# 33 places for the weighted one-hots with few signals, the counts' store beside the next tile's sums, and gathers without steps, in a two-layer graph kernel on one core

## What is computed

```
a     = h[src] @ Ws.T + h[dst] @ Wd.T + emb_rel[etype] @ Wr.T
e     = leaky_relu(a @ attn_fc2_w.T, 0.01)
w     = exp(e - segment_max(e, dst)[dst])
alpha = w / segment_sum(w, dst)[dst]
agg   = segment_sum(alpha * h[src], dst)        # h where a node has no edge
x1    = layernorm(x + agg + h @ loop_weight)
# twice, from h = x1:
msg   = (rel_embed[etype] + h[src]) @ W_r
h     = rrelu(segment_sum(msg, dst) * deg**-0.5 + where(no edge, h @ W_el, h @ W_sl))
out   = layernorm(x1 + h)
```

## Time and profile before

| | us |
|---|---|
| median of 3 runs | 2790.08 (2789.8 to 2791.62) |
| profiled execution, span from the first to the last instruction | 3256.5 |
| busy in it: PE / PEld / DVE / ACT / POOL | 2357.3 / 1900.0 / 2054.9 / 1230.7 / 1582.9 |
| its longest groups: gathers L587, comparisons L1142 of the counts, closing sums L979, sums L904 | 1537.7 / 564.1 / 551.4 / 548.8 |
| its mean granted clock of TensorE | 0.860 of full speed |

### The profile page before, as it was taken

One profiled execution on the slowest core, in us unless ns is written; L12 is line 12 of the kernel. 1 busy time (PEld: TensorE's weight loads), 2 busy tenths in 40 slices (PEclk: granted clock), 3 DMA queues, 4 the chain that ended last, 5 costly groups with the idle time before them and its releaser, 6 DMA issues.

```text
span 3256.5 us, 45435 instructions
## 1 busy us (share of the span) xinstructions
PE 2357.3 (72%) x16208; PEld 1900.0 (58%) x16208; DVE 2054.9 (63%) x4582; ACT 1230.7 (38%) x3215; POOL 1582.9 (49%) x1672
## 2 busy tenths in 40 slices
PE   1136666666766767677677777777777799999999
PEld 0125544545555556556556566566565677688887
DVE  4647766767767767767767777777676745632333
ACT  1125544444444544444444544444444432300000
POOL 4634666666666666666666666666656500000000
PEclk9877877878788888888887888888888899999999
DMA  6323444344444444454444444444444335466665
GB/s 182 113 78 112 131 136 123 118 148 128 123 155 132 121 155 133 122 156 135 125 157 135 126 141 142 140 139 129 154 130 121 93 128 170 142 214 214 210 212 168
DMA packets 184631, 463.49 MB, mean 142 GB/s; under 512 B 86337, under 2 KB 113785, under 8 KB 164578
## 3 DMA queue, kind: packets, MB, share of 16 engines
q1 hardware_dynamic: 116050, 339.10, 30.9%
q0 software_dynamic: 53600, 114.17, 14.2%
q10 hardware_dynamic: 14752, 7.26, 0.9%
HBM read 362.54 MB, written 97.84 MB: 141 GB/s over the span
## 4 chain that ended last, share of the span: by engine, by line
PE 60%; issue 12%; another core or an unknown queue 11%; DVE 8%; ACT 8%; DMA 1%; SPq 0%; ACTq 0%; DVEq 0%
PE pair L979 16%; PE bank L904 15%; PE pair L834 8%; PE bank L865 8%; DVE arena L1142 4%; ACT arena L609 4%; PE pair L811 2%; PE pair L803 2%; PE pair L801 1%; PE pair L802 1%; ACT arena L706 1%; PE pair L952 1%; ACT L653 1%; PE bank L857 1%
## 5 line engine op out<-in xcount | busy, mean ns | idle before, releaser
L587 POOL DMA_INDIRECT arena<-rows,srcw x1617 | 1537.7, 951 | 1000.7 <-issue 411.3
L1142 DVE TENSOR_TENSOR arena<-bank,idx 128x2000 bf16<-128x2000 bf16 (+3 forms) x700 | 564.1, 855 | 289.9 <-PE pair L834 218.7
L904 PE MATMUL bank<-arena 128*125 128x130 f32 x3300 | 548.8, 340 | 54.2 <-ACT arena L706 30.1
L904 PEld LDWEIGHTS bank<-arena 128*125 128x125 f32 x3300 | 534.0, 241 | 62.6 <-ACT arena L706 35.0
L979 PE MATMUL pair<-arena 125*125 125x384 bf16 x3285 | 551.4, 326 | 1.6 <-DVE arena L1343 1.6
L834 PE MATMUL pair<-arena 128*128 128x250 bf16 x2500 | 400.5, 312 | 201.7 <-issue 87.6
L609 ACT ACTIVATE arena<-pair 99x264 f32<-99x264 f32 (+2 forms) x410 | 282.3, 711 | 674.1 <-PE pair L834 306.6
L706 ACT ACTIVATE arena<-arena,wexp 128x128 f32<-128x128 bf16 x1650 | 496.1, 387 | 105.7 <-PE bank L904 61.8
L979 PEld LDWEIGHTS pair<-arena 125*125 125x125 bf16 x3285 | 447.4, 136 | 103.3 <-issue 8.4
L834 PEld LDWEIGHTS pair<-arena 128*128 128x128 bf16 x2500 | 260.2, 110 | 313.9 <-issue 187.5
L1112 DVE TENSOR_TENSOR arena<-arena,bank 128x4224 bf16<-128x4224 int16 x150 | 344.2, 2350 | 1.7
(11 more groups left out here) (250 smaller groups left out, 2329.6 us busy)
## 6 DMA issues: line engine op xcount, KB each, us to landing
arena<-counts SPq DMA_DIRECT2D x106, 812.5 KB, 4.4
counts<-arena SPq DMA_DIRECT2D x50, 1562.5 KB
arena<-dst SPq DMA_DIRECT2D x50, 1056.0 KB
arena<-etype SPq DMA_DIRECT2D x50, 1056.0 KB
arena<-rows,srcw POOLq DMA_INDIRECT x1617
arena<-counts SPq DMA_DIRECT2D x14, 281.2 KB, 2.7
edge_terms<-arena SPq DMA_DIRECT2D x200, 12.4 KB
xt<-in_x_dram SPq DMA_DIRECT2D x50, 62.5 KB
```

The costliest lines, as they stand in the source:

```text
L587: pool.indirect_dma_start(out=rows[:, q, c, :], out_offset=None, in_=rows0, in_offset=bass.IndirectOffsetOnAxis(ap=srcw[:, q, c:c + 1], ax ...
L904: r = pe.matmul(sums[0:TN, 0:D + 2], hot[:, n % RING, 0:TN], rows[:, q, c, 0:D + 2], start=(c == 0), stop=(c == C - 1))
L1142: return v.tensor_tensor(hot_.rearrange("p c (j t) -> p c j t", t=2), iotap[:, 0:w].rearrange("p (j t) -> p j t", t=2)[:, None, :, :].broa ...
```

## The change

The ring becomes a place for each column, `hot` of 33 x 128 x 128 floats, which lies over the types' one-hots `toh`. ScalarE no longer waits for a sum matmul. It signals every third one-hot (WMG = 3, so NWM = 11 signals a tile), and TensorE waits before every third column. TensorE signals 4 of the 33 sum matmuls. VectorE, before it writes the next `hotb` and `toh`, waits also for the last sum matmul. The counts' store waits until the first three one-hots of the next tile are done (but for the last two tiles). `keep_step` goes, so a tile's gathers wait for their lists and, by the last sum of two tiles before, for their buffer.

```diff
--- before.py
+++ after.py
@@ -50,7 +50,10 @@
 QB = 4
 QK = 4
 QW = WIN // (QB * QK)
-RING = 12
+WMG = 3
+NWM = C // WMG
+ACC_AT = (0, 9, 19, C - 1)
+NAC = len(ACC_AT)
 BIG = 1e30
 SHIFT = 128.0
 NBK = 2
@@ -195,11 +198,12 @@
         acc = carve([P, NT, D])
         ROWS_AT = at_[0]
         rows = carve([P, 2, C, HW])
-        hot = carve([P, RING, P])
+        TOH_AT = at_[0]
+        toh = carve([P, C, R], BF16)
+        here(TOH_AT)
+        hot = carve([P, C, P])
         HOTB_AT = at_[0]
         hotb = carve([P, C, P], BF16)
-        TOH_AT = at_[0]
-        toh = carve([P, C, R], BF16)
         LIST_AT = at_[0]
         dB = carve([P, WIN], I16)
         eB = carve([P, WIN], I16)
@@ -258,7 +262,7 @@
         viol = carve([P, EW])
         here(TOH_AT)
         prod = carve([P, XP, D])
-        assert at_[0] <= LIST_AT
+        assert at_[0] <= HOTB_AT
         here(AT_AT)
         iota_i = carve([P, 256], I32)
         thr_i = carve([P, NT + 1], I32)
@@ -461,6 +465,8 @@
 
             def store_counts(t):
                 sp.wait_ge(s("ev"), seq("cnt", t, BT - 1) + 1)
+                if t + 2 < NT:
+                    sp.wait_ge(s("wm"), NWM * (t + 1) + 1)
                 sp.dma_start(counts[t][:, 0:HI * TN], AT[:, :, :].rearrange("p h d -> p (h d)")).then_inc(s("at_stored"), 16)
                 sp.wait_ge(s("ev"), seq("turned", t) + 1)
                 sp.dma_start(counts[t][:, HI * TN:HS * TN], ctb[:, t % 2, :, :].rearrange("p h d -> p (h d)")).then_inc(s("at_stored"), 16)
@@ -534,38 +540,6 @@
                     out=rows[:, 0, c, 0:D], out_offset=None, in_=x,
                     in_offset=bass.IndirectOffsetOnAxis(ap=srcw[:, 0, c:c + 1], axis=0)).then_inc(s("gath_x"), 16)
 
-        def keep_step(pool, t, c):
-            if c == 0:
-                pool.wait_ge(s("pb"), seq("cnt", t - 2, 2) + 1)
-            if c == 2:
-                pool.wait_ge(s("pb"), seq("cnt", t - 2, 3) + 1)
-            if c == 4:
-                pool.wait_ge(s("pb"), seq("cnt", t - 2, 4) + 1)
-            if c == 6:
-                pool.wait_ge(s("pb"), seq("cnt", t - 2, 6) + 1)
-            if c == 8:
-                pool.wait_ge(s("nm"), t - 1)
...
-            if c == 32:
-                pool.wait_ge(s("pb"), seq("cnt", t - 1, 2) + 1)
-
         def pool_fast(pool):
             pool.wait_ge(s("st_rows"), ROWS_STORED)
             for t in range(1, NT):
@@ -580,10 +554,8 @@
                             in_=rec.rearrange("(a j) r -> a j r", j=GW),
                             in_offset=bass.IndirectOffsetOnAxis(ap=gidx[:, b:b + 1], axis=1)).then_inc(s("ld_rec%d" % b), 16)
                 if t >= 2:
-                    pool.wait_ge(s("acc_c"), C * (t - 1))
+                    pool.wait_ge(s("acc_c"), NAC * (t - 1))
                 for c in range(C):
-                    if t >= 3:
-                        keep_step(pool, t, c)
                     pool.indirect_dma_start(
                         out=rows[:, q, c, :], out_offset=None, in_=rows0,
                         in_offset=bass.IndirectOffsetOnAxis(ap=srcw[:, q, c:c + 1], axis=0)).then_inc(s("gath%d" % q), 16)
@@ -700,10 +672,9 @@
                 act.activation(wexp[:, 0:C], z[:, 0:C], ACT.Exp).then_inc(s("w_ready"), 1)
                 act.wait_ge(s("w_ready"), t + 1)
                 for c in range(C):
-                    n = t * C + c
-                    if n >= RING:
-                        act.wait_ge(s("acc_c"), n - RING + 1)
-                    act.activation(hot[:, n % RING, :], hotb[:, c, :], ACT.Copy, scale=wexp[:, c:c + 1]).then_inc(s("wm"), 1)
+                    r = act.activation(hot[:, c, :], hotb[:, c, :], ACT.Copy, scale=wexp[:, c:c + 1])
+                    if c % WMG == WMG - 1:
+                        r.then_inc(s("wm"), 1)
                 if t - 1 in EARLY:
                     act.wait_ge(s("early_read"), EARLY_TILES.index(t - 1) + 1)
                     act.nop().then_inc(s("ev"), 1)
@@ -896,13 +867,14 @@
                 pe.matmul(bank[0][:, 2 * P + 1:2 * P + 2], cfb[0:1, 1, :], ones[0:1, 0:1], start=True, stop=True).then_inc(s("cf_ps"), 1)
                 if t >= 1:
                     pe.wait_ge(s("fin"), t)
-                pe.wait_ge(s("wm"), t * C + 1)
+                pe.wait_ge(s("wm"), NWM * t + 1)
                 degree(t)
                 for c in range(C):
-                    n = t * C + c
-                    pe.wait_ge(s("wm"), n + 1)
-                    r = pe.matmul(sums[0:TN, 0:D + 2], hot[:, n % RING, 0:TN], rows[:, q, c, 0:D + 2], start=(c == 0), stop=(c == C - 1))
-                    r.then_inc(s("acc_c"), 1)
+                    if c % WMG == 0:
+                        pe.wait_ge(s("wm"), NWM * t + c // WMG + 1)
+                    r = pe.matmul(sums[0:TN, 0:D + 2], hot[:, c, 0:TN], rows[:, q, c, 0:D + 2], start=(c == 0), stop=(c == C - 1))
+                    if c in ACC_AT:
+                        r.then_inc(s("acc_c"), 1)
                 if t + 1 < NT:
                     terms(t + 1)
                 if 1 <= t < NT - 1:
@@ -1150,7 +1122,8 @@
                 v.tensor_copy(et2[:], etw[:, q, :][:, :, None].broadcast_to([P, C, 2]))
                 link(v.tensor_scalar(dstB[:], dstw[:, q, :], -BIG, None, ALU.mult))
                 if t >= 1:
-                    v.wait_ge(s("wm"), C * t)
+                    v.wait_ge(s("wm"), NWM * t)
+                    v.wait_ge(s("acc_c"), NAC * t)
                     v.wait_ge(s("pb"), seq("types", t - 1) + 1)
                 paired(hotb, dl2, C)
                 paired(toh, et2, C).then_inc(s("hot_ready"), 1)
@@ -1193,7 +1166,7 @@
 
             def finalize(t):
                 a, yt = sums, yr[0:TN, t % 2, :]
-                v.wait_ge(s("acc_c"), C * (t + 1))
+                v.wait_ge(s("acc_c"), NAC * (t + 1))
                 v.tensor_scalar(iso[0:TN, t:t + 1], a[0:TN, D + 1:D + 2], 0.5, None, ALU.is_lt)
                 v.tensor_scalar(niso[0:TN, t:t + 1], a[0:TN, D + 1:D + 2], 0.5, None, ALU.is_ge)
                 v.tensor_scalar(nv[0:TN, 0, 1:2], a[0:TN, D + 2:D + 3], 1.0, None, ALU.max)
```

More of the change, by code:

```diff
@@ L535, in pool_shared @@
                     in_offset=bass.IndirectOffsetOnAxis(ap=srcw[:, 0, c:c + 1], axis=0)).then_inc(s("gath_x"), 16)
-        def keep_step(pool, t, c):
-            if c == 0:
-                pool.wait_ge(s("pb"), seq("cnt", t - 2, 2) + 1)
-            if c == 2:
-                pool.wait_ge(s("pb"), seq("cnt", t - 2, 3) + 1)
-            if c == 4:
-                pool.wait_ge(s("pb"), seq("cnt", t - 2, 4) + 1)
-            if c == 6:
-                pool.wait_ge(s("pb"), seq("cnt", t - 2, 6) + 1)
-            if c == 8:
-                pool.wait_ge(s("nm"), t - 1)
-            if c == 10:
-                pool.wait_ge(s("th_ps"), t)
-            if c == 12:
-                pool.wait_ge(s("cf_ps"), t)
-            if c == 15:
-                pool.wait_ge(s("acc_c"), C * (t - 1) + 1)
-            if c == 17:
-                pool.wait_ge(s("acc_c"), C * (t - 1) + 10)
-            if c == 19:
-                pool.wait_ge(s("acc_c"), C * (t - 1) + 20)
-            if c == 22:
-                pool.wait_ge(s("acc_c"), C * t)
-            if c == 24:
-                pool.wait_ge(s("pb"), seq("dr", t, QK - 1) + 1)
-            if c == 28:
-                pool.wait_ge(s("pd0"), t - 1)
-            if c == 30:
-                pool.wait_ge(s("pb"), seq("cnt", t - 1, 1) + 1)
-            if c == 32:
-                pool.wait_ge(s("pb"), seq("cnt", t - 1, 2) + 1)
         def pool_fast(pool):
```

## The result

The changed kernel takes 2777.94 us (median of 4 runs, 2776.1 to 2778.76), the kernel before 2790.24 (4 runs, 2789.8 to 2791.62). The ratio is 0.9953, with a 95% interval of 0.9941 to 0.9965: 12.3 us, or 0.47%, faster. The profiled run took 2776.1 us, with a span of 2774.0 us and a mean granted clock of 0.906.

A forecast was written before the change was run, and what follows sets the result against it. The prediction took the tile loop to be bound by its chain of waits, with no engine full. From 2790 us it took 15 for the store and 15 for the gathers and added 13 for the sums' later start: 2773 us, range 2712 to 2822.

The forecast's parts named there:

- The gathers, -15 us: POOL's gathers: without their 15 waits a tile they may start 15 us earlier, spent once; bounds 0 and -15.
- The cover that I gave VectorE's new wait: VectorE's wait for the last sum ends 2.8 us before its next operation, 2.3 with the later start.
- I take that most lateness belongs to the profiled execution, and a small rest to every run.: TensorE's late signals in the loop: about 9 us a tile when profiled, 0.3 to 0.5 in plain runs.
- The store, -15 us: Counts' store moved beside the sums: removes some 0.3 us a tile of lateness in plain runs; bounds 0 and 30.
- 33 places, few signals, 0: ScalarE's ring and the sum and weight signals: worth 0 in an undisturbed tile; signals bounded by 0 and 0.3 us.
- The late start of the sums, +13 us: TensorE's sums wait for three one-hots, 0.58 us later, which costs in 23 tiles; bounds 0 and 28.
- The span, some 3030 us: Profiled span of the changed kernel: 3256 less 240 for the store plus 13 for the later start.
- Tile 27 without its late signals, 40.0 us: One tile of the loop: 48.95 us less the late signals' 3.9, 1.05, 2.2 and 1.8 leaves 40.0.
- (b): Rival: unbroken gathers on POOL starve TensorE's signals; 2862 with half the tiles, 2934 us with all; chance 0.11.
- (a): Rival: lateness is the profile's alone, POOL isn't the bound, the later sums decide; 2803 to 2818 us; chance 0.24.
- (c): Rival: plain runs have the store's stall at a third or more; 2710 us and below; chance 0.08.
- (d): Rival: the terms cancel, or the change does nothing outside the profile; 2785 to 2796 us; chance 0.21.

The follow-up runs named there:

- e0_before: The kernel before, unedited, run and profiled again: 2790.98 us, span 2788.9 us.
- e1_steps: The changed kernel with the 15 waits a tile put back into the gathers: 2791.21 us, ratio to the kernel before 1.0004.
- e2_store_early: The changed kernel with the counts' store issued where it was before the change: 2777.8 us, ratio to the kernel before 0.9956.
- e4_before_free: The kernel before with only POOL's 15 waits inside each tile removed: 2774.9 us, ratio to the kernel before 0.9952.
- e8_one_wait: The changed kernel with one wait put back, at the first gather of tile 3: 2791.28 us, ratio to the kernel before 1.0005.
- e3_all_signals: The changed kernel with a signal for every one-hot and every sum matmul, still 33 places: 2775.35 us, ratio to the kernel before 0.9947.
- e6_30: The changed kernel with 30 of 33 gathers a tile from tile 3 on: 2723.35 us, ratio to the kernel before 0.9767.

## Why the prediction was right or wrong

The time, 2773 forecast and 2777.94 measured, was right within 0.2%, and in the likeliest case; the 4505 us of a late chip are far outside the range. The gain has its cause in the one term that holds, the gathers. That the sum comes so near is luck: the other two terms, -15 for the store and +13 for the later start, both measured 0 and nearly cancel.

- **The gathers, -15 us.** Right in mechanism and sign, and nearly in size, though the step had it as one of two readings and for the early tiles alone. POOL's cycle, 41.3 us a tile, is the bound from tile 3 on, and the lead is spent once. The 40.3 us that seemed to speak against it were the median less 158 and 616 us, both from the late profile, over 50 tiles; in e0_before the gathers of tiles 3 to 49 run from 194.65 to 2138 us at 41.3 a tile, and preparation takes 120. Within their jobs it is 13.4 us (e1_steps less e2_store_early), 14.5 (e4_before_free against the kernel before) and 16.4 (e8_one_wait less e4_before_free, which differ in the rest of the change as well). The step looked for it as 15 us in tile 27; it arises at tile 3 alone, as 11.0 + 2.4 us. The cover that I gave VectorE's new wait was never at issue, since VectorE waits 4 us for rows later in the tile.
- **"I take that most lateness belongs to the profiled execution, and a small rest to every run."** This is the step that failed. Lateness is neither: a prompt chip has none, by its times, in any of 30 runs of the kernel before, a late chip has all of it in each of 22, within 1% of 3250. The two numbers that I subtracted, 3256.5 and 2790.08, must have come from two kinds of chip (where the trace shown of before was taken isn't on record, but within no job do runs of that kernel show both times), and what a median "has left" of the lateness had no meaning. The Trainium skill, "NOTIFIC — the notification-queue block", section "7.1 Overflow: three behaviours, one of which stalls the engine", had led me to make it a matter of recording; it gives the stalled producer as one of three settings of a full queue, and no run here shows which is set or a time without records. That the same kernel differs by 460 us between chips is nothing that this rule tells apart.
- **The store, -15 us.** Measured 0 (e2_store_early). With no lateness on a prompt chip there was nothing to take. On a late chip the rows above speak against the store as the cause of the 3.9 us: gathers alone hold signals back longer, and the stall of the earlier trace rows ended in a pause of POOL. The Trainium skill, "SBUF — State Buffer", section "Who interferes with whom", had it that a DMA does not contend with a compute engine, and by it the term was 0: e2_store_early, which moves the store at no gain or loss, agrees with the page, against my reading of the stall.
- **33 places, few signals, 0.** Measured 0 within 2.4 us (e3_all_signals, e1_steps); e4_before_free, which has neither, gains 14.5 us where the change gains 12.3. The 26.3 ns a signal of the Trainium skill, "TensorE: Matmul & The Clock Gate", section "The cost: per-tile semaphore tail", would have made 37 us with the 29 signals of the sums; e3_all_signals has them all and is not slower, so no such tail shows beside one-hots that set the pace.
- **The late start of the sums, +13 us.** Measured 0. I laid it on TensorE's path from tile 27 on, but my own first term said that POOL is the bound, and then every such 0.58 us is hidden: two steps of one sum contradicted each other. Its size was nearer the mark: in most tiles the end of the sums moves by nearly 0.5 us (10.78 against 10.29 us after the first one-hot), where the step had 0.58 and at least some 0.4.
- **The span, some 3030 us.** Measured 2774.0 on a prompt chip and 4495.7 on a late one; it was neither.
- **Tile 27 without its late signals, 40.0 us.** This step fits, as far as a mean over tiles can say: e6_30, where the other engines' chain is the bound in the later tiles, takes 40.3 us a tile.

**The rivals.** (b) is what the traces show on a late chip: while POOL gathers without a pause, TensorE's signals come late, in every tile. I had priced it at a tenth of the lateness or more, up to 2934, and kept it for "plain runs". Its own formula at the full lateness of such a chip, 30 x 48 = 1440 us, is 15% above the 1254 measured. In the profiles the stretch from the first gather of tile 3 to the last of tile 49 takes 3528.8 us instead of 2329.5, 1199 more, and the way from there to the end another 52. Its evidence was in hand; what I lacked was the thought that all of a machine's runs may be so. (a), (c) and (d) did not occur.

## What to carry to other kernels

When a profile and the medians of the same kernel differ by far more than runs do, don't split the difference over terms: run the kernel before again first, and on more than one chip. Waits that look like slack on a full engine may be what lets another engine's signals through. Here removing them gains 12 us on one kind of chip, and the change that removes them loses 1254 on the other, so on the runs of this case it should not be taken as it is; whether it is harmless there with its 15 waits kept, no run shows. And where one engine issues without a gap, a kernel's time moves only by its issues and by its first start: ask of each part of a change whether it touches these two.

## What the runs showed of the hardware

- Jobs, each on a chip of its own, differ in this: with the same program, the same 944 ns a gather and the same 606 us of closing matmuls, TensorE's signals come at once on two chips and up to tens of microseconds late on two others, for as long as POOL issues gathers. Which resource they share stays open; that TensorE's own matmuls thin out as well (one in 2 or 3 us, "issue") says that more than the signal is held back. The granted clock falls with it, 0.743 against 0.906 over the span, as TensorE idles.
- A gather of 128 rows takes POOL 0.94 us and 0.30 to the next, for 16 bytes a row as for 528.
- A signal after each sum matmul, 29 more a tile, and one after each weighted one-hot, 22 more, cost nothing that the ranges tell (2775.35 us with them, 2777.8 to 2777.94 without).
